# Head outputs brought to feature rows by DMA, and query/key rows laid in quarters, in a fused attention and coupling-net kernel

## The chip, the cores and the metric

One core of one Trainium2 chip runs the whole program. The metric is device time in microseconds (us), as the median of the runs shown. Five engines run their own instruction streams and meet at semaphores: PE (TensorE), ACT (ScalarE), DVE (VectorE), POOL (GpSimd), and SP (SyncE), which here does nothing but issue DMAs and wait.

## What is computed

The input x is 16 batches of 1024 tokens with 256 features. For each batch:

```python
x = x + layernorm(attention(layernorm(x)))      # 16 heads of 8 features, on the first 128 features
x = x + layernorm(coupling(layernorm(x)))

# attention: q, k, v = left @ W.T ; energy = q.k / 4 ; att = softmax over keys ; out = att @ v ; out @ Wo.T + bo
# coupling, 3 cycles, gf from the mean over tokens:
#   tf  = sigmoid(gelu(gelu(gelu(out@w1+b1)@w2+b2)@w3+b3)@w4+b4)
#   out = out + (0.1 + ar * (0.7*gf + 0.3*tf - 0.5) * 2) * twist(out)
```

The weights of the projections are scaled up, so the softmax needs its row maxima, and q and k are split into three bf16 parts each (high, middle, low) to keep fp32 accuracy on the bf16 path of PE.

## The kernel before, in words

The main loop runs b from -2 to 17 over batches, in the same order on each engine. Each turn has two stages, and they are software-pipelined over batches.

**Attention stage of batch b**, 64 steps (`STEPS`), that is 8 groups of 8 steps. A group is one half of the queries (h) and four heads (g). In a step PE computes transposed scores for four heads (L409, bf16, contraction over 48 rows of split parts and 3 rows that carry minus the row maximum), ACT takes the exponential of them (L599, two instructions of 128x1024), and PE weighs the values with them (L424). Column 9 of each head's values is one, so the sum of the exponentials comes out beside the 8 features. At the end of a group ACT copies the 128x512 result to `headsT` (`take_heads`, L608): partition 32*i+d holds feature d of head i of the group, partition 32*i+8 its sum.

**Coupling stage**, 30 beats (`BEATS`). Beat j runs one layer of the coupling net of batch b-1 on PE and its activation on ACT (three cycles of ten layers, `coupling`, `layer_out`). Between them stand, at hand-written beats: for batch b+2 the layernorm (`STATS0`, `NORM0`), projections (`PROJECT_QK`, `PROJECT_V`) and the split into parts; for batch b the way from `headsT` to the projected output (`HEADS`, `TURN_TOK`, `WO`), its layernorm, and the turn into `state`; for batch b-2 the turn back, layernorm and store (`BACK`, `STATS3`, `NORM3`, `ADD_OUT`).

**The way from headsT to the output projection** (batch b, beats 0 to 7): `turn_heads` transposes eight token tiles, four 128x128 fp32 transposes each (L453). For each tile `divide` on DVE takes a reciprocal of the 16 sums (L843) and multiplies the tile with them (L847). `turn_tok` transposes the tiles back (L461, two halves of four), `take_tok` on ACT copies them to `feat_h` (L664), and `project_out` multiplies with `wo` (L468).

**The maxima.** For every query block of every head the row maximum is found ahead of its attention: a *unit* is one matmul 48x128 by 48x512 (L391) and one maximum over 512 columns on DVE (L814). There are 256 units in a batch, 32 in a group. They run as filler: 3 in each attention step (4 in batch 0), and as `BEAT_UNITS` says in the beats, 20, 23 and 21 in the three cycles. They lead the attention by `LEAD` = 112 units, batch 0 by `LEAD0` = 52, which are done before the first attention starts. After a group's 32 units DVE joins and POOL cuts the maxima into three bf16 parts (L963 to L966), and SP transposes them by DMA and writes them into `q_rows` (`lay_max_rows`: one DMA transpose, a wait for its landing, four DMAs), when unit 32(gi+1)+`LAY_AFTER` passes. The scores of a group wait for them (`max_rows_laid`).

**The rows.** `q_rows` and `k_rows` hold the split parts, 8 rows for each of 6 terms, on partitions 0 to 47 (side 0) and 64 to 111 (side 1). They are laid from `parts` by DMA: `lay_row`, L278, one DMA in each of the first 48 steps of the attention before, 64 KB each. The first batch's are laid in `lay_first_rows`: 36 DMAs from SP (L291) and 12 from ACT (L645), in halves of eight heads; the first unit waits for the first half (24 DMAs).

SP's program is one queue in program order: rows, maxima, loads and stores of x. A wait in it holds back everything behind it. The rest of PE's PSUM banks go round as a ring (`ring_bank`): 3 in attention, 5 in the coupling stage, shared by the units and all small results.

## Time and profile before

| | us |
|---|---|
| median of 3 runs | 3556.51 (3555.34 to 3559.84) |
| the profiled execution's own time | 3557.75 |
| its span in the trace | 3555.8 |

```profile
PE   4999999999999999999999999999999999999996
DVE  5998989888898988989888897988989888898821
ACT  2767979798897979889798897979889797896974
PEclk6998999999999999999999999999999999999998
```

The digits are the busy share of 40 equal slices of the span in tenths, and in PEclk the clock granted to TensorE in tenths of full speed. The kernel has a short opening, then a pattern that repeats every 212 us or so (an attention stage of about 130 us, a coupling stage of about 82 us), and an end in which only the coupling net of the last two batches is left.

### The profile page before, as it was taken

To read this page: it belongs to the slowest core of one execution; us is meant where nothing else is said; L and a number is where in the kernel's file an instruction comes from. 1 tells how busy PE (TensorE), PEld (TensorE's weight loads), DVE (VectorE), ACT (ScalarE), POOL (GpSimd) and SP (SyncE) were. 2 spreads that over 40 slices of the span, in tenths; PEclk is the share of its full clock that TensorE was granted. 3 is DMA by queue.
4 is the path that set the end of the run, shared out by engine and by line. 5 is a ranking of instruction groups with operands and counts; after the bars stand their busy time and mean duration, and the time that the engine had idled before them with its cause. 6 is when DMAs were issued, how large, how long until landed. Compare 5 with 4: busy or idle time off the path is not lost.

```text
span 3555.8 us, 56168 instructions
## 1 busy us (share of the span) xinstructions
PE 3379.5 (95%) x19968; PEld 1008.8 (28%) x19968; DVE 2981.2 (84%) x5677; ACT 2931.5 (82%) x3868; POOL 972.2 (27%) x1353
## 2 busy tenths in 40 slices
PE   4999999999999999999999999999999999999996
PEld 1222232323324232232323224232232323223232
DVE  5998989888898988989888897988989888898821
ACT  2767979798897979889798897979889797896974
POOL 3002050421505133060421405033050422404034
PEclk6998999999999999999999999999999999999998
DMA  3101102021211202111020211202111020211001
GB/s 85 27 24 44 33 30 34 26 54 23 51 26 33 54 18 55 30 45 32 26 54 22 51 37 27 49 26 46 30 48 28 26 55 22 44 32 26 3 24 36
DMA packets 71957, 127.89 MB, mean 36 GB/s; under 512 B 37120, under 2 KB 38528, under 8 KB 63616
## 3 DMA queue, kind: packets, MB, share of 16 engines
q1 hardware_dynamic: 68896, 106.75, 12.8%
q0 software_dynamic: 2304, 16.78, 2.6%
q8 instruction: 160, 2.62, 0.3%
q10 hardware_dynamic: 480, 0.79, 0.1%
q14 instruction: 117, 0.96, 0.1%
HBM read 34.61 MB, written 33.55 MB: 19 GB/s over the span
## 4 chain that ended last, share of the span: by engine, by line
PE 72%; DVE 10%; ACT 9%; issue 4%; POOL 2%; DMA 0%; SPq 0%; ACTq 0%; POOLq 0%; DVEq 0%
PE heads_ps L424 24%; PE ring_ps L391 15%; PE scoresT_ps L409 11%; PE scoresT_ps L521 10%; DVE max_parts L814 8%; ACT p_sb L599 4%; PE scoresT_ps L526 3%; DVE stats L825 1%; ACT headsT L608 1%; PE ring_ps L453 1%; PE scoresT_ps L529 1%; PE scoresT_ps L532 1%; POOL y_sb L985 1%; PE scoresT_ps L391 1%; POOL couple L1008 1%
## 5 line engine op out<-in xcount | busy, mean ns | idle before, releaser
L814 DVE TENSOR_REDUCE max_parts<-ring_ps 128x1 f32<-128x512 f32 x3704 | 2343.5, 684 | 269.5 <-PE ring_ps L391 210.5
L599 ACT ACTIVATE p_sb<-scoresT_ps 128x1024 f32<-128x1024 f32 x2048 | 1969.8, 1024 | 103.3 <-PE scoresT_ps L409 79.5
L424 PE MATMUL heads_ps<-p_sb,v_sb 128*9 128x512 f32 x8192 | 1080.4, 599 | 17.9 <-ACT headsT L608 11.9
L391 PE MATMUL ring_ps<-k_rows,q_rows 48*128 48x512 bf16 x3704 | 1074.6, 387 | 17.7 <-DVE max_parts L814 6.3
L409 PE MATMUL scoresT_ps<-q_rows,k_rows 51*128 51x512 bf16 x4096 | 1030.5, 386 | 18.7 <-ACT p_sb L599 9.1
L391 PEld LDWEIGHTS ring_ps<-k_rows,q_rows 48*128 48x128 bf16 x3704 | 263.2, 94 | 1272.6 <-DVE max_parts L814 1177.6
L963 POOL CAST max_wide<-max_all 128x16 bf16<-128x16 f32 x128 | 25.3, 198 | 1709.4 <-DVE max_all L820 1706.7
L521 PE MATMUL scoresT_ps<-state,w 128*128 128x512 f32 x768 | 383.6, 623 | 4.0 <-DVE state L865 2.0
L719 ACT ACTIVATE p_sb<-scoresT_ps,b 128x512 f32<-128x512 f32 x192 | 131.7, 686 | 210.7 <-PE scoresT_ps L521 210.5
L409 PEld LDWEIGHTS scoresT_ps<-q_rows,k_rows 51*128 51x128 bf16 x4096 | 209.4, 94 | 253.4 <-ACT p_sb L599 221.0
L424 PEld LDWEIGHTS heads_ps<-p_sb,v_sb 128*9 128x9 f32 x8192 | 124.5, 88 | 292.1 <-issue 281.6
L526 PE MATMUL scoresT_ps<-p_sb,w 128*128 128x512 f32 x384 | 189.2, 615 | 12.8 <-ACT p_sb L719 11.3
L985 POOL TENSOR_TENSOR y_sb<-y_sb,bo 128x512 f32<-128x512 f32 x64 | 87.5, 1368 | 412.8 <-ACT y_sb L669 412.8
L521 PEld LDWEIGHTS scoresT_ps<-state,w 128*128 128x128 f32 x768 | 132.2, 191 | 170.6 <-issue 162.2
L814 DVE TENSOR_REDUCE max_parts<-scoresT_ps 128x1 f32<-128x512 f32 x187 | 126.7, 678 | 46.3 <-PE scoresT_ps L391 46.3
L721 ACT ACTIVATE p_sb<-scoresT_ps,b 128x512 f32<-128x512 f32 x96 | 66.0, 687 | 98.8 <-PE scoresT_ps L526 98.7
L612 ACT ACTIVATE x_in<-x_in,offset,rstd 128x128 f32<-128x128 f32 (+1 forms) x256 | 123.9, 537 | 22.8 <-POOL offset L973 14.1
L814 DVE TENSOR_REDUCE max_parts<-heads_ps 128x1 f32<-128x512 f32 x205 | 139.1, 678 | 0.4 <-PE heads_ps L391 0.4
L825 DVE BATCH_NORM_STATS2 stats<-x_in 128x6 f32<-128x256 f32 x256 | 94.6, 413 | 37.9 <-ACT x_in L689 29.3
L532 PE MATMUL scoresT_ps<-p_sb,w_all 64*128 64x512 f32 x192 | 102.2, 612 | 13.3 <-ACT p_sb L723 13.3
L1016 POOL TENSOR_TENSOR state<-state,couple 128x512 f32<-128x512 f32 x64 | 98.9, 1546 | 34.7 <-DVE couple L857 34.2
L971 POOL TENSOR_TENSOR rstd<-rstd,minus_half 128x8 f32<-128x8 f32 x64 | 106.9, 1670 | 5.3
(166 smaller groups left out, 2869.5 us busy)
## 6 DMA issues: line engine op xcount, KB each, us to landing
q_rows<-parts SPq DMA_DIRECT2D x378, 64.0 KB
k_rows<-parts SPq DMA_DIRECT2D x378, 64.0 KB
x_sb<-in_x SPq DMA_DIRECT2D x16, 1024.0 KB, 4.8
out<-x_sb SPq DMA_DIRECT2D x16, 1024.0 KB, 3.9
out<-x_in POOLq DMA_DIRECT2D x16, 1024.0 KB, 7.9
x_in<-in_x SPq DMA_DIRECT2D x15, 1024.0 KB, 5.4
q_rows<-max_rows SPq DMA_DIRECT2D x512, 3.0 KB
max_rows<-max_wide SPq DMA_TRANSPOSE x128, 2.3
```

The costliest lines, as they stand in the source:

```text
L391: e.matmul(ring_bank(max_taken, u + 1), q_rows[rows, slot, pair, h * BANK + qb * P:h * BANK + (qb + 1) * P], k_rows[rows, slot, pair, kh * ...
L409: m = e.matmul(scoresT_ps[:, (2 * two + side) * BANK:(2 * two + side + 1) * BANK], k_rows[rows, slot, pair, kb * P:(kb + 1) * P], q_rows[r ...
L424: m = e.matmul(heads_ps[32 * j:32 * j + DH + 1, :], v_sb[:, b % 2, kb, 4 * (group % NG) + j, 0:DH + 1], p_sb[:, n % 2, j, :], start=(kb == ...
L521: o = e.matmul(ps, w1[:, k, m * P:(m + 1) * P], state[:, b % 2, k, c * BANK:(c + 1) * BANK], start=(k == 0), stop=(k == 1))
L526: o = e.matmul(ps, w2[:, k, :], p_sb[:, 0, 2 * c + k, :], start=(k == 0), stop=(k == 1))
L532: o = e.matmul(ps, w4_all[:, :], p_sb[0:D // 2, 1, 2 + c, :], start=True, stop=True)
L599: e.activation(p_sb[:, n % 2, 2 * two:2 * two + 2, :].rearrange("p h n -> p (h n)"), scoresT_ps[:, 2 * two * BANK:(2 * two + 2) * BANK], A ...
L612: m = e.activation(dst(t), src(t), ACT.Identity, bias=offset[i][:, t:t + 1], scale=rstd[i][:, t:t + 1])
L719: e.activation(p_sb[:, 0, 2 * c + m, :], ps, ACT.Gelu, bias=b1[:, m:m + 1]).then_inc(hid_done, 1)
L814: e.tensor_reduce(max_parts[:, gi % 2, kh, col:col + 1], bank_of(max_taken, u + 1), AX.X, ALU.max).then_inc(max_taken, 1)
L825: m = e.bn_stats(stats[i][:, t, :], src(t))
L985: e.tensor_tensor(y_sb[:, rows, :], y_sb[:, rows, :], bo[:, :].unsqueeze(1).to_broadcast([P, 2, E]), ALU.add).then_inc(y_done, 1)
```

## The change

- **Heads.** `turn_heads`, `turn_tok`, `take_tok` and the eight `divide` steps go. SP copies the features from `headsT` straight into `feat_h` by DMA after each group (`lay_heads`, four DMAs of 16 KB, five when the half is complete: the fifth gathers the 32 KB of sums into `sums_in`). At beat `INVERT` = 2 DVE takes one reciprocal of 64x256. SP spreads the result over the partitions (`lay_sums`, four DMAs of 128 KB written). At beats `DIVIDE` = 4, 5 DVE multiplies the two halves of `feat_h`, 128x512 each. The rows of `wo` are permuted on the host to match. `WO` moves from beats 3, 4, 6, 7 to 5, 5, 6, 6.
- **Rows.** They are laid in quarters (four heads) instead of halves: `lay_row` issues 96 DMAs of 32 KB in 64 steps instead of 48 of 64 KB in 48 steps. The units wait for their own quarter.
- **Opening.** `lay_first_rows` goes by quarters: 54 DMAs from SP, 18 from ACT, 24 from POOL. The first unit waits for the first quarter (18 from SP, 6 from ACT). `LEAD0` goes from 52 to 60, and these units stand in beats 5 to 20 instead of 5 to 29.
- **Schedule.** `BEAT_UNITS` gives 18, 24 and 22 units to the cycles; `LAY_AFTER` goes from 3 to 6. `BACK`, `STATS3`, `ROOT3`, `NORM3`, `ADD_OUT`, `ROOT0`, `ROOT1`, `NORM1`, `ADD1` and the second twist (`TWIST1`) stand one or two beats earlier; `STATE` two later, `PROJECT_V` two and three later, `ROOT2` one later.

```diff
-LAY_AFTER = 3
+SUM_PARTS = 2
+SUM_ROWS = H * SUM_PARTS
+LAID = 16 * (2 * H + NH)
+LAY_AFTER = 6
...
-BEAT_UNITS = (3, 2, 2, 1, 3, 2, 2, 2, 2, 1,
-              2, 2, 2, 3, 3, 2, 2, 4, 2, 1,
-              2, 1, 2, 3, 4, 2, 2, 2, 2, 1)
+BEAT_UNITS = (4, 1, 2, 1, 2, 1, 2, 2, 1, 1,
+              2, 3, 2, 3, 3, 2, 2, 4, 2, 1,
+              2, 1, 2, 3, 4, 2, 2, 2, 3, 1)
-LEAD0 = 52
+LEAD0 = 60
+ACT_GROUPS, POOL_GROUPS = (0, 1), (2, 3)
-LAST_BEAT, LAST_STEP = 28, 0
+LAST_BEAT, LAST_STEP = 27, 1
-STATS0, ROOT0, NORM0, TURN_X = (0, 1, 2, 3), 4, (5, 6, 7, 8), (8, 9)
-PROJECT_QK, SPLIT, PROJECT_V = (17, 18, 23, 24), (20, 21, 26, 27), (20, 26)
+STATS0, ROOT0, NORM0, TURN_X = (0, 1, 2, 3), 3, (5, 6, 7, 8), (8, 9)
+PROJECT_QK, SPLIT, PROJECT_V = (17, 18, 23, 24), (20, 21, 26, 27), (22, 29)
-BACK, STATS3, ROOT3, NORM3, ADD_OUT = (10, 11, 12, 13), (11, 12, 13, 14), 15, (17, 18, 19, 25), 27
-HEADS, TURN_TOK, WO, STATS1, ROOT1 = (0, 0, 0, 0, 1, 2, 3, 4), (1, 5), (3, 4, 6, 7), (4, 5, 7, 8), 9
-NORM1, ADD1, STATS2, ROOT2 = (11, 12, 13, 14), (12, 13, 14, 15), (14, 16, 17, 18), 18
-NORM2, STATE = (21, 22, 23, 24), (24, 25, 26, 27)
-GLOBAL = (1, 3, 5)
-TWIST0, UPDATE0, TWIST1, UPDATE1 = 6, 7, 10, 10
+BACK, STATS3, ROOT3, NORM3, ADD_OUT = (8, 9, 10, 11), (10, 11, 12, 13), 14, (16, 17, 20, 24), 26
+INVERT, DIVIDE, WO, STATS1, ROOT1 = 2, (4, 5), (5, 5, 6, 6), (6, 6, 7, 7), 7
+NORM1, ADD1, STATS2, ROOT2 = (10, 11, 12, 13), (11, 12, 13, 15), (14, 16, 17, 18), 19
+NORM2, STATE = (21, 22, 23, 24), (26, 27, 28, 29)
+GLOBAL = (0, 3, 5)
+TWIST0, UPDATE0, TWIST1, UPDATE1 = 6, 7, 9, 10
...
+            def lay_heads(b, group):
+                h, g = divmod(group, NG)
+                e.wait_ge(heads_evac, GROUPS * b + group + 1)
+                if b and group == 0:
+                    e.wait_ge(wo_done, 4 * b)
+                    e.wait_ge(divided, 2 * b)
+                if g == NG - 1:
+                    e.dma_start(sums_in[SUM_ROWS * h:SUM_ROWS * (h + 1), :],
+                                headsT[DH:P:32, h, :, :]).then_inc(heads_laid, 16)
+                for i in range(4):
+                    at = 32 * i + DH * g
+                    e.dma_start(feat_h[at:at + DH, h * BANK:(h + 1) * BANK],
+                                headsT[32 * i:32 * i + DH, h, g, :]).then_inc(heads_laid, 16)
+            def lay_sums(b):
+                e.wait_ge(inverted, b + 1)
+                for h in range(NH):
+                    for k in range(SUM_PARTS):
+                        at = h * BANK + k * BANK // SUM_PARTS
+                        rows = sums_in[SUM_ROWS * h + k:SUM_ROWS * (h + 1):SUM_PARTS, :]
+                        e.dma_start(sums_h[:, at:at + BANK // SUM_PARTS],
+                                    rows.unsqueeze(1).to_broadcast([H, DH, BANK // SUM_PARTS])).then_inc(sums_laid[h], 16)
...
-                    if 0 <= b < N - 1 and n < 48:
-                        lay_row(b + 1, n)
+                    if 0 <= b < N - 1:
+                        for at in range(3 * n // 2, 3 * (n + 1) // 2):
+                            lay_row(b + 1, at)
+                    if valid(b) and n and n % NT == 0:
+                        lay_heads(b, n // NT - 1)
                 for j in range(BEATS):
+                    if valid(b) and j == 0:
+                        lay_heads(b, GROUPS - 1)
+                    if valid(b) and j == INVERT:
+                        lay_sums(b)
...
+            def invert(b):
+                e.wait_ge(heads_laid, LAID * (b + 1))
+                e.reciprocal(sums_in[:, :], sums_in[:, :]).then_inc(inverted, 1)
+            def divide(b, h):
+                half = feat_h[:, h * BANK:(h + 1) * BANK]
+                e.wait_ge(sums_laid[h], 16 * SUM_PARTS * (b + 1))
+                e.tensor_tensor(half, half, sums_h[:, h * BANK:(h + 1) * BANK], ALU.mult).then_inc(divided, 1)
```

## Rows read from the trace of the kernel before

**Rows 1.** The page, part 1: busy time, share of the span, instructions.
```profile
PE 3379.5 (95%) x19968; PEld 1008.8 (28%) x19968; DVE 2981.2 (84%) x5677; ACT 2931.5 (82%) x3868; POOL 972.2 (27%) x1353
```
**Rows 2.** Busy time by stretch: stretch, length, engines, PEclk, DMA share, GB/s.
```profile
1152.00:1283.00 131.00, 129.00 (x956) 27.12 (x956) 121.74 (x199) 126.41 (x138) 16.16 (x34) 0.99 0.24 50
1283.00:1365.00 82.00, 79.28 (x300) 34.91 (x294) 64.94 (x158) 57.29 (x107) 44.49 (x52) 1.00 0.06 18
```
**Rows 3.** The same view: the three cycles of that stage, then two late ones.
```profile
1283.90:1312.90 29.00, 28.81 (x123) 14.57 (x119) 21.41 (x57) 16.15 (x31) 11.05 (x13) 1.00 0.00 1
1312.90:1338.70 25.80, 24.93 (x82) 9.89 (x83) 25.11 (x65) 18.62 (x34) 18.06 (x20) 1.00 0.11 43
1338.70:1364.60 25.90, 24.50 (x92) 10.40 (x90) 17.15 (x34) 22.11 (x45) 15.06 (x19) 1.00 0.06 7
3402.30:3427.40 25.10, 24.23 (x101) 13.44 (x98) 8.23 (x24) 12.86 (x22) 7.98 (x7) 1.00 0.00 1
3470.70:3490.50 19.80, 17.63 (x43) 6.69 (x43) 1.39 (x2) 9.05 (x16) 11.35 (x10) 0.95 0.10 20
```
**Rows 4.** Groups of instructions by line and shape: busy, mean ns, idle before.
```profile
L453 PE MATMUL ring_ps<-ident,headsT 128*128 128x128 f32 x380 | 52.8, 275 | 0.0
L843 DVE RECIPROCAL recip<-ring_ps 128x16 f32<-128x16 f32 x95 | 24.4, 257 | 78.0 <-PE ring_ps L453 74.8
L847 DVE TENSOR_TENSOR tok_h<-ring_ps,recip 128x128 f32<-128x128 f32 x95 | 27.7, 292 | 3.3
L865 DVE TENSOR_TENSOR state<-state,couple 128x512 f32<-128x512 f32 x64 | 44.2, 691 | 15.3 <-POOL couple L1008 12.3
```
**Rows 5.** Timeline at one coupling stage's start: start, us, engine, line, count.
```profile
1284.01 0.60 ACT L608 ACTIVATE headsT<-heads_ps 128x512 f32<-128x512 f32 x1 [1.17 <-PE heads_ps L424]
...
1285.69 1.47 PE L453 MATMUL ring_ps<-ident,headsT 128*128 128x128 f32 x12
...
1287.00 0.60 PE L453 MATMUL scoresT_ps<-ident,headsT 128*128 128x128 f32 x4
...
1287.54 0.39 PE L391 MATMUL heads_ps<-k_rows,q_rows 48*128 48x512 bf16 x1
```
**Rows 6.** Waits of SP's queue: who, for whom, us in total, times, longest.
```profile
SPq L256 <- POOL max_wide L966: 1645.4, 128, 33.6
```
**Rows 7.** Timeline of SP's queue within an attention stage.
```profile
1230.80 1.12 SPq L256 DMA_TRANSPOSE max_rows<-max_wide  x1
1233.12 3.02 SPq L263 DMA_DIRECT2D q_rows<-max_rows  x4
1236.18 7.17 SPq L278 DMA_DIRECT2D q_rows<-parts  x10
```
**Rows 8.** DMA issues: line, engine, count, KB each, median us to landing.
```profile
x_sb<-in_x SPq DMA_DIRECT2D x16, 1024.0 KB, 4.8
max_rows<-max_wide SPq DMA_TRANSPOSE x128, 2.3
```
**Rows 9.** Timeline of the opening, from the first row DMA to the first exponential.
```profile
24.03 2.35 SPq L291 DMA_DIRECT2D q_rows<-parts  x3
...
38.37 0.68 ACTq L645 DMA_DIRECT2D k_rows<-parts  x1
...
51.22 0.67 SPq L291 DMA_DIRECT2D k_rows<-parts  x1
...
52.15 0.60 PE L391 MATMUL scoresT_ps<-k_rows,q_rows 48*128 48x512 bf16 x1 [25.25 <-DMA k_rows<-parts]
...
87.95 1.02 ACT L599 ACTIVATE p_sb<-scoresT_ps 128x1024 f32<-128x1024 f32 x1 [3.09 <-PE scoresT_ps L409]
```
**Rows 10.** Busy time by stretch: the 52 opening units, attention 0, the stage behind.
```profile
52.10:87.90 35.80, 33.36 (x87) 10.31 (x87) 30.15 (x51) 8.80 (x16) 9.94 (x12) 0.50 0.31 62
87.90:250.60 162.70, 152.09 (x1014) 33.80 (x1013) 159.66 (x267) 127.76 (x135) 6.72 (x32) 0.97 0.12 29
250.60:307.20 56.60, 47.12 (x176) 20.10 (x175) 49.90 (x126) 26.18 (x56) 27.87 (x36) 0.73 0.11 39
```
**Rows 11.** Groups by line: a DMA issued from POOL.
```profile
L1088 POOL DMA_DIRECT2D out<-x_in x16 | 15.3, 954 | 29.0 <-ACT x_in L612 29.0
```

More of the change, by code:

```diff
@@ L286, in lay_first_rows @@
                         if i:
[L288 to L292 removed]
+                            e.wait_ge(const_pool, 4)
+                            e.wait_ge(ones_laid, 1)
+                        for side in range(2 if (g, part) == (0, 0) else 1):
+                            for n in (n for n, term in enumerate(TERMS) if term[i] == part):
+                                top, source = 64 * side + DH * n, 64 * side + 16 * g
+                                e.dma_start((q_rows, k_rows)[i][top:top + DH, 0, 2 * g:2 * g + 2, :],
+                                            parts[source:source + 16, i, part, :]).then_inc(rows_laid[0][g], 16)
             for i in range(4):
@@ L340, in sync_program @@
                         load_x(1)
[L341 to L343 removed]
+                        for g in range(NG):
+                            lay_first_rows(g)
                     if valid(b) and j == 0:
@@ L446, in project_v @@
                 m.then_inc(v_done, 1)
-            def turn_heads(b, t):
-                h = t // TPH
-                e.wait_ge(heads_evac, b * GROUPS + (h + 1) * NG)
-                ps = misc_bank(divided, NT * b + t + 1)
-                for g in range(NG):
-                    m = e.transpose(ps[:, g * P:(g + 1) * P], headsT[:, h, g, t % TPH * P:(t % TPH + 1) * P],
-                                    ident[:, :])
-                m.then_inc(headT_done, 1)
-            def turn_tok(b, h):
-                e.wait_ge(divided, NT * b + (h + 1) * TPH)
-                ps = misc_bank(feath_ready, 2 * b + h + 1)
-                for t in range(h * TPH, (h + 1) * TPH):
-                    m = e.transpose(ps[:, t % TPH * P:(t % TPH + 1) * P], tok_h[:, t, :], ident[:, :])
-                m.then_inc(tokT_done, 1)
             def project_out(b, j):
-                e.wait_ge(feath_ready, 2 * b + j // 2 + 1)
+                e.wait_ge(divided, 2 * b + j // 2 + 1)
                 ps = misc_bank(y_taken, 4 * b + j + 1)
@@ L578, in tensor_program @@
                     if valid(b):
-                        if j in TURN_TOK:
-                            turn_tok(b, TURN_TOK.index(j))
-                        for t in range(NT):
-                            if j == HEADS[t]:
-                                turn_heads(b, t)
-                        if j in WO:
-                            project_out(b, WO.index(j))
+                        for i in range(4):
+                            if j == WO[i]:
+                                project_out(b, i)
                         if j in STATE:
@@ L626, in take_qk @@
                     slot = (b - 1) % 2
-                    for half in range(2):
-                        e.wait_ge(rows_laid[slot][half], 24 * 16 * ((b - 1) // 2 + 1))
+                    for g in range(NG):
+                        e.wait_ge(rows_laid[slot][g], laid(b - 1, g))
+                        if g in POOL_GROUPS:
+                            e.wait_ge(pool_laid[g], 12 * 16)
                 if i == 1:
@@ L634, in take_qk, with lay_first_rows @@
                 e.activation(parts[:, i, 0, cols], ps, ACT.Copy).then_inc(qk_evac, 1)
-            def lay_first_rows():
-                for part in range(3):
+            def lay_first_rows(g):
+                for part in range(0 if g else 1, 3):
                     for i in range(2):
@@ L999, in split_low, with lay_first_rows @@
                                 ALU.subtract).then_inc(low_done, 1)
+            def lay_first_rows(g):
+                e.wait_ge(low_done, 4)
+                e.wait_ge(ones_laid, 1)
+                for i in range(2):
+                    for n in range(len(TERMS)):
+                        e.dma_start((q_rows, k_rows)[i][64 + DH * n:64 + DH * n + DH, 0, 2 * g:2 * g + 2, :],
+                                    parts[64 + 16 * g:80 + 16 * g, i, TERMS[n][i], :]).then_inc(pool_laid[g], 16)
             def twist(b, cycle, c):
@@ L1089, in gpsimd_program @@
                     if valid(b):
-                        if j in WO:
-                            add_bias(b, WO.index(j))
+                        for i in range(4):
+                            if j == WO[i]:
+                                add_bias(b, i)
                         if j == ROOT1:
```

97 lines of the change are left out of this document (41 added, 56 removed).

## The prediction

> **What bounds the kernel now.** I read the busy shares first: PE 95%, DVE 84% [rows 1]. An average over unlike stages says little, so the next view is the busy time by stretch. In an attention stage of 131 us PE is busy for 129.0, ACT for 126.4, DVE for 121.7; in the 82 us coupling stage PE for 79.3, DVE for 64.9, ACT for 57.3 [rows 2]. Attention is the longer stage, but the change takes nothing from PE there. The coupling stage is where it works, so I cut that stage into its three cycles [rows 3]. The first third (29.0 us) is PE alone: 28.8 busy against 21.4 on DVE. The second (25.8 us) has DVE busy for 25.1, PE for 24.9: DVE is the bound there, or very near. The third (25.9 us) has PE at 24.5, with gaps in which PE waits for the next activation of the coupling net's own chain. The last two rows of [rows 3] say how far such a cycle can shrink: with the head turns but no units and no projections of a later batch the first cycle takes 25.1 us, and with nothing but the coupling net and the small global net 19.8. Within the first third, twelve and then four transposes of `turn_heads` stand between 1285.69 and 1287.54 [rows 5]. SP is idle for long times: 1645 us of its queue's time is waiting for POOL's cut of the maxima [rows 6]. In the opening the first unit on PE waits for row DMAs until 52.15 [rows 9].
>
> **The heads, PE's side.** Sixteen transposes take 1.85 us (1285.69 to 1287.54), 0.116 each by their spacing, not the 275 ns of a single one, which overlap [rows 4, 5]. A batch has 32 of them and 8 of `turn_tok` of the same shape: 40 x 0.116 = 4.6 us of PE in each first third. WO's matmuls stay. Two `turn_back` (4 transposes each, 0.46 us) move from the second third into the first: +0.9 there. Two units fewer, at 0.2 to 0.39 us each (0.39 is one with its fill, [rows 5]): -0.4 to -0.8. So some 4.2 us less PE work of 28.8. Not all of it becomes time: from the two early-stage rows, 19.8 us with little filler and 29.0 with all of it, PE busy 17.6 and 28.8, so (29.0-19.8)/(28.8-17.6) = 0.82 us of time for 1 us of PE work [rows 3]. That is -3.4 us.
>
> **The heads, the new chain.** In its place stands: copy of the last `headsT` (ends 0.74 us after the stage's first matmul, which was at 1283.87) [rows 5], five DMA issues, landing, reciprocal, four issues, landing, multiply. SP issues ten row DMAs in 7.17 us, 0.72 each [rows 7]. A small DMA lands 2.3 us after its issue starts (the transpose); the 1 MB one 4.8 [rows 8]. Counted from the first matmul of the stage: issues start at 0.9, the last starts at 3.8, has landed by 6.5 (by the two landings, 6.1 and 8.6). DVE is then still at the five units and three statistics of beats 0 to 2, until about 8, so the reciprocal waits for nothing; but if SP is late by over 1.5 us, DVE stands still. The reciprocal's price is not in the trace at this size. Lower bound: 256 elements at the rate of the 128x512 multiply, 691/512 = 1.35 ns each, 0.35 us and a start of 0.1. Upper bound: sixteen times the 257 ns of the one with 16 elements, 4.1 us. The 128-element multiply at 292 ns leaves 0.12 for the start (292 - 128 x 1.35), so the 16-element reciprocal spends 0.137 on 16, 8.6 ns each, and 256 cost 2.2 + 0.1 = 2.3 us; this I take [rows 4]. It ends at 10.4; `lay_sums` issues two DMAs per half: the first half has landed at 11.2 + 2.3 = 13.5 (up to 16 if 128 KB lands like the 1 MB load), the second 1.4 later. Multiplying: 0.7 us per half. PE reaches WO at about 14 by the sum of its work in beats 0 to 5: a wait of 0.3 to 0.8 us is likely. I add 0.6.
> On the Trainium skill's page VectorE: DVE Perf Modes, section on the 8-slice pipeline, reciprocal is an iterative division with a repeat count of 8. At eight times 1.35 ns its 256 elements would cost 2.8 us instead of 2.3, and the sum would be worse by 0.5 us a batch; my two rows point the same way but don't measure it.
>
> **DVE's side.** Out: 8 x (0.257 + 0.292) = 4.4 us a batch [rows 4]. In: 2.3 + 2 x 0.7 = 3.7. Even, in a third where DVE has 7.6 us to spare. ACT loses two copies. Nothing comes of either.
>
> **The units and the moved steps.** The second third gets one unit more, and DVE is its bound. A unit costs DVE 0.636 us (162.7 us for 256 in attention 0, DVE busy 98%) [rows 10]: +0.6. The second twist moved to beats 9 and 19 leaves one in and one out; its wait for the coupling's scaling is now in front of the next beat's unit, cover: five banks of units. `STATE` and `PROJECT_V` move into beats 26 to 29, where PE has its gaps (1.4 us in this third): up to -1.4, less one unit more: -0.2 taken.
> Sum of a full stage: -3.4 + 0.6 + 0.6 - 0.2 = -2.4; with the gaps better filled at either end -3.2. I take -2.7 and keep -5 and +0.5 for the range. Fourteen coupling stages lie between attention 1 and attention 15: -38 us.
>
> **SP's queue.** It gets 48 row DMAs and 38 head and sum DMAs more in each batch. In eight attention steps (16.1 us): 12 rows x 0.72 = 8.6, one `lay_heads` 4 x 0.72 = 2.9, and in six of eight intervals a `lay_max_rows` of 1.12 + 1.2 wait + 3.0 = 5.3 [rows 7]. Together 16.8 where there is one, 11.5 where there is none. So SP is nearly full, and each `lay_heads` ties it to the steps by its wait for `heads_evac`; queued behind that wait are rows and, what counts, the maxima. The tightest is group 7's: it is issued in step 50, behind `lay_heads` of group 5 (free about 1 us into step 48) and three rows: landed at 1 + 2.9 + 2.2 + 5.3 + 2.3 = 13.7 us after step 48 began, and scores need it at 16.1. Margin 2.4 us, cost nothing. At the stage's end SP is 1 to 2 us late at worst, which the 1.5 us of cover for the reciprocal just takes. The load of `x_sb` goes behind `lay_heads` and is needed ten beats later. The earlier `ADD_OUT` frees SP at the stage's start about one beat sooner.
> The Trainium skill's page DMA: Bandwidth & Descriptors (Bandwidth) speaks against this part: transfers under 64 KB are dominated by their descriptors (measured there on loads from HBM, which these are not), and this change cuts 64 KB pieces into 32 and adds ones of 16. By that rule each half-size transfer would cost nearly the same, which is also what I get from the issue time; what it would do here is the first rival below.
>
> **The opening.** 18 SP issues and 6 ACT issues stand before the first unit, instead of the first halves' 24 that were issued by 39.05 and waited for until 52.15 [rows 9]. SP's 18 take 24.0 to about 37 (the wait for the split parts is inside), landing with some of the backlog that made 13 us before: 39 to 44. I take 41: first unit 11 us earlier. 60 units at 0.6 and the projections of batch 1 behind them instead of between them (about 7 us of PE at 1.2 GHz, the granted clock 0.50 of [rows 10], DVE dry for 4 of it): the first exponential at 86.5 instead of 87.95, -1.4, with 8 units more done. Attention 0 is DVE-bound and keeps its 256 units. The stage behind has 52 units instead of 60: 8 x 0.636 = -5.1, but it has no coupling net to fill the time, so the new chain (heads landed at 6.5, sums at 13.5) shows: DVE stands still for 3 to 5 us. -1 taken, -6 and +3 kept. POOL issues 24 DMAs at 0.954 [rows 11], 23 us, after `row_rstd`; the next it has to do is the cut of group 0 at about 60, and it is free by 58. Worth up to 3 us if late.
>
> **The end.** The stage behind attention 15 has beats of 2 us, so the sums come late: of the 4.6 us nearly all is given back to the wait; -1. The rest is unchanged.
>
> **Sum.** -38 - 1.4 - 1 - 1 = -41 from 3557.75 gives 3516.4 for such an execution; the median lies 1.2 below it: **3515**.
>
> **Rivals.** (a) *SP's queue is the new bound*, slower. If a row or head DMA costs not 0.72 but over about 0.85, the intervals with maxima take 19 us of 16.1, and the last `lay_heads` starts 3 us late. DVE then waits at the reciprocal, PE at its ring banks; each us late is a us per stage, 15 times. At 0.95 (POOL's price) 4 more us late, minus the 2.7 gained: about +1.5 x 15, 3578. For: SP is full by count. Against: the four small ones of 3 KB cost 0.72 too, so the price hardly depends on the size, and a smaller one should not cost more. 12%. (b) *The sums are late everywhere*: landing of 128 KB spread costs 4.8 and the reciprocal 4.1; PE waits 3 us more at WO, and of 2.7 nothing to 1 is left: 3545 to 3555. 15%. (c) *The first quarter isn't early*: the transfers are bound by the data path, not by the issue; the opening gives nothing or loses 4: 3521. 10%, within the forecast's range. (d) *More of the saved PE time counts*, -4.2 a stage, and the third cycle's gaps close: 3490. 15%. (e) The forecast itself, 3503 to 3530: 48%.
>
> A measurement here can tell about 0.2% (7 us) from no change. Faster by over that: (c), (d), (e) and most of (b): 0.82. Within: 0.05. Slower: 0.13. The range: from 3486 (d) to 3549 (b).
>
> **What would show it.** Right: no L453 and L461 rows; the first cycle at 25.5 to 26.5 us instead of 29.0, the second at 26 to 26.5, the third at 25 to 26; attention stages unchanged at 129 to 131.5; the reciprocal at 2.3 us; the first unit at 41. Wrong: a wait of L409 for a DMA at step 56 or attention stages over 132 us (a), DVE idle before the reciprocal or before the multiply by more than 1 us, PE idle before L468 (b), or more half-clock stretches at attention starts, since PE has less to do in the first third.

## The result and the profile after

The changed kernel takes 3465.98 us (median of 4 runs, 3463.11 to 3468.58) against 3555.93 us of the kernel before (median of 4): ratio 0.9745, 95% interval 0.9728 to 0.9762. It is 90 us faster. The forecast was 41 us, and its range ended at 3486: right in its sign, and less than half of what came.

The page of the profiled execution (busy time, clock by slices):

```profile
span 3462.1 us, 55776 instructions
PE 3286.2 (95%) x19328; PEld 932.0 (27%) x19328; DVE 2938.1 (85%) x5469; ACT 2911.6 (84%) x3836; POOL 986.1 (28%) x1377
...
PEclk7998999999999999999999999999999999999998
```

PE has 93.3 us less to do (3379.5 in [rows 1]) and the span is 93.7 us shorter: PE's share stays at 95%. The same views by stretch as [rows 2] and [rows 3]: an attention stage, the coupling stage behind it, its three cycles, and the first cycle of the last two nets. A cycle ends here, as in [rows 3], where ACT starts the activation of the cycle's last layer (stretch, length, PE, PEld, DVE, ACT, POOL busy, PEclk, DMA share, GB/s):

```profile
1123.00:1254.40 131.40, 129.54 (x966) 28.61 (x965) 122.40 (x201) 128.01 (x143) 14.46 (x33) 1.00 0.17 42
1254.40:1331.30 76.90, 74.06 (x260) 30.14 (x260) 61.96 (x144) 56.08 (x106) 47.99 (x54) 1.00 0.20 53
1255.40:1281.60 26.20, 24.63 (x87) 10.92 (x84) 20.28 (x52) 15.24 (x29) 11.98 (x13) 1.00 0.25 71
1281.60:1304.90 23.30, 22.88 (x77) 8.50 (x76) 22.65 (x53) 18.04 (x33) 16.59 (x20) 1.00 0.12 47
1304.90:1329.60 24.70, 23.93 (x84) 9.71 (x84) 17.39 (x38) 21.09 (x39) 17.72 (x21) 1.00 0.17 29
3312.70:3335.30 22.60, 20.62 (x65) 9.53 (x62) 8.45 (x21) 12.00 (x21) 8.78 (x8) 1.00 0.27 75
3374.70:3395.40 20.70, 18.00 (x51) 6.90 (x50) 1.81 (x4) 9.20 (x17) 10.85 (x10) 1.00 0.03 5
```

The first cycle went from 29.0 to 26.2, the second from 25.8 to 23.3, the third from 25.9 to 24.7. Unrounded the three shrink by 6.3 us together, but the stage from 82.2 to 76.95, by 5.3 only: between the last activation and the first exponential of the attention 0.57 us became 1.62. ACT there, before:

```profile
1364.50 0.67 ACT L733 ACTIVATE couple<-scoresT_ps,b_half 128x512 f32<-128x512 f32 x1
1365.07 1.93 ACT L599 ACTIVATE p_sb<-scoresT_ps 128x1024 f32<-128x1024 f32 x2
```

and after, with the copies of the values and of the last state now in between:

```profile
1329.73 0.68 ACT L756 ACTIVATE couple<-scoresT_ps,b_half 128x512 f32<-128x512 f32 x1
1330.30 0.60 ACT L686 ACTIVATE v_sb<-heads_ps 128x512 f32<-128x512 f32 x1
1330.78 0.60 ACT L705 ACTIVATE state<-scoresT_ps 128x512 f32<-128x512 f32 x1
...
1331.34 1.95 ACT L627 ACTIVATE p_sb<-scoresT_ps 128x1024 f32<-128x1024 f32 x2
```

The mean of the fourteen full coupling stages, part by part:

| part of a full stage | before | after | difference | forecast |
|---|---|---|---|---|
| last exponential to first matmul | 1.03 | 1.03 | 0 | 0 |
| first cycle | 28.96 | 26.15 | -2.8 | -3.4 + 0.6 |
| second cycle | 25.54 | 23.30 | -2.2 | +0.6 |
| third cycle | 25.79 | 24.64 | -1.15 | -0.2 |
| last activation to next exponential | 0.57 | 1.58 | +1.0 | 0 |
| better filled gaps at either end | | | | -0.3 |
| stage | 81.89 | 76.70 | -5.2 | -2.7 |

Laid end to end by the first and last exponential of each batch, the two spans differ so:

| stretch | before | after | difference | forecast |
|---|---|---|---|---|
| start to first exponential | 87.9 | 86.3 | -1.6 | -1.4 |
| attention 0 | 162.7 | 158.6 | -4.1 | 0 |
| stage behind attention 0 | 56.6 | 53.4 | -3.2 | -1 |
| attention 1 to 15 together | 1947.6 | 1939.5 | -8.1 | 0 |
| the 14 full coupling stages | 1146.4 | 1073.8 | -72.6 | -38 |
| behind attention 15 | 154.5 | 150.4 | -4.1 | -1 |
| span | 3555.8 | 3462.1 | -93.7 | -41 |

The full coupling stages hold 35 of the 53 us that were missed, attention 0 to 15 another 12. DVE's timeline around the edge between the first and second cycle of a stage, before:

```profile
1309.83 0.75 DVE L825 BATCH_NORM_STATS2 stats<-y_sb 128x6 f32<-128x256 f32 x2 [1.16 <-POOL y_sb L985]
...
1313.41 0.74 DVE L825 BATCH_NORM_STATS2 stats<-y_sb 128x6 f32<-128x256 f32 x2
1314.18 0.64 DVE L835 BATCH_NORM_AGGREGATE moments<-stats 128x2 f32<-128x6 f32 x8
...
1317.89 1.43 DVE L857 TENSOR_TENSOR couple<-couple,state 128x512 f32<-128x512 f32 x1
```

and after, where the second cycle begins at 1281.6:

```profile
1263.02 1.73 DVE L862 RECIPROCAL sums_in<-sums_in 64x256 f32<-64x256 f32 x1
...
1267.84 0.69 DVE L867 TENSOR_TENSOR feat_h<-feat_h,sums_h 128x512 f32<-128x512 f32 x1
...
1269.65 0.68 DVE L867 TENSOR_TENSOR feat_h<-feat_h,sums_h 128x512 f32<-128x512 f32 x1
...
1279.09 0.75 DVE L847 BATCH_NORM_STATS2 stats<-y_sb 128x6 f32<-128x256 f32 x2 [0.50 <-POOL y_sb L1007]
1279.87 0.64 DVE L857 BATCH_NORM_AGGREGATE moments<-stats 128x2 f32<-128x6 f32 x8
```

Before, the statistics of the attention output ended inside the second cycle (which began at 1312.9), in front of its units. After, they end before it. The reciprocal waits for nothing here (no bracket behind it), and PE's first two WO products at 1270.16 stand right behind the small global net (`hg`, 1269.86): the new chain costs PE no wait in this stage. SP's queue in the same stage:

```profile
1222.17 0.67 SPq L317 DMA_DIRECT2D k_rows<-parts  x1
1224.56 2.67 SPq L292 DMA_DIRECT2D feat_h<-headsT  x4
...
1253.52 4.30 SPq L317 DMA_DIRECT2D q_rows<-parts  x6
1257.87 0.58 SPq L288 DMA_DIRECT2D sums_in<-headsT  x1
1258.49 2.69 SPq L292 DMA_DIRECT2D feat_h<-headsT  x4
1261.29 0.38 SPq L396 DMA_DIRECT2D x_sb<-in_x  x1
```

From 1224.56 to 1261.67 it has no gap over 0.15 us except the landing of the maxima. The last heads' DMAs start at 1257.87, 2.4 us after the stage's first matmul (1255.43), because row DMAs stand in front of them. The heads were ready 0.7 us after that matmul.

### The profile page after: what moved, and what is told of

Same layout as the page of the kernel before. It is cut to its first block, busy times and chain, and to the rows that moved or that the text cites. A ratio compares the mean times of both kernels' runs of the same rounds, so it can differ in the third digit from the quotient of the medians.

```text
span 3462.1 us, 55776 instructions
## 1 busy us (share of the span) xinstructions
PE 3286.2 (95%) x19328; PEld 932.0 (27%) x19328; DVE 2938.1 (85%) x5469; ACT 2911.6 (84%) x3836; POOL 986.1 (28%) x1377
## 3 DMA queue, kind: packets, MB, share of 16 engines
q1 hardware_dynamic: 93072, 124.03, 13.6%
## 4 chain that ended last, share of the span: by engine, by line
PE 71%; DVE 13%; ACT 9%; issue 4%; SPq 2%; POOL 1%; DMA 1%; POOLq 0%; DVEq 0%
PE heads_ps L472 24%; PE ring_ps L439 15%; PE scoresT_ps L457 11%; DVE max_parts L836 10%; PE scoresT_ps L553 8%; ACT p_sb L627 4%; PE scoresT_ps L558 3%; PE scoresT_ps L561 2%; DVE stats L847 2%; PE scoresT_ps L564 1%; ACT headsT L636 1%; PE ring_ps L500 1%; PE scoresT_ps L486 1%; PE heads_ps L439 1%; ACT p_sb L742 1%
## 5 line engine op out<-in xcount | busy, mean ns | idle before, releaser
L439 PE MATMUL ring_ps<-k_rows,q_rows 48*128 48x512 bf16 x3741 | 1078.1, 385 | 24.1 <-DVE max_parts L836 14.2
L472 PE MATMUL heads_ps<-p_sb,v_sb 128*9 128x512 f32 x8192 | 1073.9, 596 | 17.9 <-ACT headsT L636 11.9
L985 POOL CAST max_wide<-max_all 128x16 bf16<-128x16 f32 x128 | 25.1, 196 | 1769.1 <-DVE max_all L842 1769.1
L836 DVE TENSOR_REDUCE max_parts<-scoresT_ps 128x1 f32<-128x512 f32 x144 | 97.9, 680 | 36.0 <-PE scoresT_ps L439 35.9
L561 PE MATMUL scoresT_ps<-p_sb,w 128*64 128x512 f32 x192 | 101.9, 612 | 15.3 <-ACT p_sb L744 13.7
L992 POOL TENSOR_SCALAR rstd<-moments 128x8 f32<-128x8 f32 x64 | 23.5, 367 | 303.2 <-DVE moments L857 300.0
```

The lines of the kernel that those rows point to most:

```text
L439: e.matmul(ring_bank(max_taken, u + 1), q_rows[rows, slot, pair, h * BANK + qb * P:h * BANK + (qb + 1) * P], k_rows[rows, slot, pair, kh * ...
L472: m = e.matmul(heads_ps[32 * j:32 * j + DH + 1, :], v_sb[:, b % 2, kb, 4 * (group % NG) + j, 0:DH + 1], p_sb[:, n % 2, j, :], start=(kb == ...
L561: o = e.matmul(ps[0:D // 2, :], w3[:, :], p_sb[:, 1, c, :], start=True, stop=True)
L836: e.tensor_reduce(max_parts[:, gi % 2, kh, col:col + 1], bank_of(max_taken, u + 1), AX.X, ALU.max).then_inc(max_taken, 1)
```

## The experiments

Below, "stage" is a full coupling stage, from the last exponential of one batch to the first of the next, and "attention" an attention stage. Both are the median over the batches, 76.9 and 129.0 us in the changed kernel. Cycles are read as above; one turn is one batch. A time of a single run is called so.

**The old beats in the changed kernel.**

```diff
-BEAT_UNITS = (4, 1, 2, 1, 2, 1, 2, 2, 1, 1,
-              2, 3, 2, 3, 3, 2, 2, 4, 2, 1,
-              2, 1, 2, 3, 4, 2, 2, 2, 3, 1)
+BEAT_UNITS = (3, 2, 2, 1, 3, 2, 2, 2, 2, 1,
+              2, 2, 2, 3, 3, 2, 2, 4, 2, 1,
+              2, 1, 2, 3, 4, 2, 2, 2, 2, 1)
-BACK, STATS3, ROOT3, NORM3, ADD_OUT = (8, 9, 10, 11), (10, 11, 12, 13), 14, (16, 17, 20, 24), 26
+BACK, STATS3, ROOT3, NORM3, ADD_OUT = (10, 11, 12, 13), (11, 12, 13, 14), 15, (17, 18, 19, 25), 27
-NORM2, STATE = (21, 22, 23, 24), (26, 27, 28, 29)
+NORM2, STATE = (21, 22, 23, 24), (24, 25, 26, 27)
...
```

> The changed kernel with the beats of the kernel before put back (BEAT_UNITS, GLOBAL, BACK, STATS3, NORM3, ROOT0, NORM1, ADD1, STATE, PROJECT_V, TWIST1, LAST_BEAT); head outputs still go by DMA, rows still in quarters, and DIVIDE, WO, STATS1, ROOT1 stay at their new beats since they hang on the new chain. Theory T (the saving of 5.3 us a coupling stage has several sources: PE's 40 transposes, about 2.8 us in the first cycle; DVE's statistics of the attention output taken before the second cycle instead of within it, about 1.5 us there; the new beats of the turn back, twist, state and values, about 1.5 us in all): stage of 78 to 79 us instead of 76.9, total 3485 to 3500. Rival R (removing the head turns alone carries it, the new beats are only tidying): stage 76.9 to 77.3, total within 7 us of 3466. Rival S (the new beats carry most of it): stage 80 or more, total 3510 or more.

3493.89 us, ratio 0.9827 (0.9812 to 0.9842). Stage 78.4: theory T's place. But the parts were not as T had them: the first cycle fell to 24.9, by 4.1 us, and the second stayed at 26.05 although the statistics stood early. Its three cycles:

```profile
1885.71:1910.60 24.89, 24.22 (x84) 10.38 (x81) 20.50 (x54) 14.91 (x29) 11.61 (x13) 1.00 0.26 73
1910.60:1936.65 26.05, 24.92 (x82) 9.75 (x83) 23.75 (x56) 18.62 (x33) 17.39 (x21) 1.00 0.11 43
1936.65:1962.50 25.85, 24.44 (x93) 10.46 (x91) 17.11 (x35) 22.06 (x44) 15.00 (x19) 1.00 0.06 7
```

In the second cycle DVE's work fell from 25.1 [rows 3] to 23.75 and the time did not follow: PE has 24.9 there. So in the kernel before DVE was not the only bound of that cycle.

**The new beats in the kernel before.**

```diff
-BACK, STATS3, ROOT3, NORM3, ADD_OUT = (10, 11, 12, 13), (11, 12, 13, 14), 15, (17, 18, 19, 25), 27
+BACK, STATS3, ROOT3, NORM3, ADD_OUT = (8, 9, 10, 11), (10, 11, 12, 13), 14, (16, 17, 20, 24), 26
...
```

> The kernel before (head turns on PE, rows in halves, old opening) with the new beats alone: BEAT_UNITS, GLOBAL, BACK, STATS3, NORM3, ADD_OUT, ROOT0, NORM1, ADD1, ROOT2, STATE, PROJECT_V, TWIST1, LAST_BEAT; WO and STATS1 stay at their old beats. Theory T: first cycle 29.5 (two turns back move in), second 25 to 25.8 (its DVE still begins with the last statistics of the attention output), third 24.7: stage of 80.5 to 81.5, total 3530 to 3548. Rival R: no gain, total 3550 to 3560. Rival S: stage of 79 or less, total 3515 or less.

3571.74 us, ratio 1.0047 (1.0030 to 1.0064): slower by 16 us, outside all three expectations. The second and third cycle shrink about as T said (24.9 and 24.75), but the first grows to 31.0:

```profile
1925.84:1956.80 30.96, 29.25 (x127) 15.21 (x124) 21.23 (x59) 16.23 (x31) 11.45 (x13) 1.00 0.00 1
```

With the head turns still in it, that cycle doesn't take the two turns back without loss. The fourteen stages get 24.5 us longer in all, while attention 1 to 15 gets 11.6 us shorter (1936.0 against 1947.6); in six of these stages the granted clock also fell to 1.2 GHz for 3.4 us some 8 us in, which it did in none before. Set side by side, the heads (and rows) alone give -62 us, the beats alone +16, both together -90. The beats are worth -28 where PE has been emptied first. One difference goes with the heads in this account: `WO` and the statistics behind it are early in the first of these two runs and late in the second, since they hang on the new chain.

**The same, with the global net at its old beats.** I took the crowded beat 0 (6.45 us instead of 4.17) for the cause.

```diff
-GLOBAL = (0, 3, 5)
+GLOBAL = (1, 3, 5)
```

> The kernel before with the new beats alone, as in the run that was 16 us slower, but with the global net at its old beats 1, 3, 5. Theory G (the new beat 0 is too full beside four head turns: global net and five units ask for ring banks that DVE frees one by one, PE idle 1.5 us at 4.7 us): beat 0 at 4.2 to 5.3 us instead of 6.45, first cycle 29 to 30 instead of 31.0, total 3540 to 3560. Rival: it is the two turns back moved into a cycle where PE is full anyway: first cycle 30.5 or more, total above 3563.

3573.35 us in one run, first cycle 30.98 again, beat 0 at 6.05. My theory G fell; the rival's numbers came. What remains different in that cycle are above all the turns back and the order of the units, and no run separates these two.

**The statistics late.**

```diff
-INVERT, DIVIDE, WO, STATS1, ROOT1 = 2, (4, 5), (5, 5, 6, 6), (6, 6, 7, 7), 7
+INVERT, DIVIDE, WO, STATS1, ROOT1 = 2, (4, 5), (5, 5, 6, 6), (7, 8, 9, 9), 9
```

> The changed kernel with the statistics of the attention output on DVE moved from beats 6, 6, 7, 7 to 7, 8, 9, 9 and ROOT1 from 7 to 9, nothing else. Theory T (the second cycle is bound by DVE, and it got shorter because these statistics no longer run over into it): second cycle 24.5 to 25.3 us instead of 23.3, stage 78 to 79. Rival R: DVE is not what counts there, cycles change by under 0.4 us.

3485.02 us (one run, 19 above). First and third cycle unchanged (26.2, 24.75), second 24.6 instead of 23.35, stage 78.2. The second cycle:

```profile
1284.03:1308.63 24.60, 22.97 (x77) 8.41 (x76) 23.42 (x62) 18.07 (x33) 16.73 (x18) 1.00 0.11 45
```

PE has as little to do as in the changed kernel (22.9), DVE 0.8 us more: DVE's side does count in the second cycle once PE is out of the way, as theory T said.

**The turns back late.**

```diff
-BACK, STATS3, ROOT3, NORM3, ADD_OUT = (8, 9, 10, 11), (10, 11, 12, 13), 14, (16, 17, 20, 24), 26
+BACK, STATS3, ROOT3, NORM3, ADD_OUT = (10, 11, 12, 13), (11, 12, 13, 14), 15, (17, 18, 19, 25), 27
```

> The changed kernel with BACK, STATS3, ROOT3, NORM3, ADD_OUT at the old beats only. Theory T (the second cycle has PE and DVE both full, and moving two turns back out of it took 0.9 us of PE from it, put into the first where PE has idle places): first cycle 25.2 to 25.6 instead of 26.2, second 24.8 to 26 instead of 23.3, stage 77.5 to 78.3. Rival U (the second cycle is shorter for the earlier twist or the statistics alone): second cycle within 0.4 us of 23.3 and the stage shorter than 76.9.

3489.15 us (one run, 23 above). Second cycle 26.1, first 25.85, third 24.0, stage 78.6: rival U falls, and the effect is a little larger than theory T's ranges. The second cycle:

```profile
1906.86:1932.97 26.11, 24.74 (x83) 9.71 (x84) 24.12 (x56) 18.62 (x34) 17.69 (x21) 1.00 0.11 43
```

PE 24.7 instead of 22.9 us, but DVE too has 24.1 instead of 22.65. Put together, the runs give the second cycle in all four cases:

| second cycle, us | turns back late | turns back early |
|---|---|---|
| statistics late | 25.8 (before) | 24.6, and 24.9 with the head turns on PE |
| statistics early | 26.1, with all old beats 26.05 | 23.35 (changed kernel) |

The early statistics alone give nothing, the early turns back alone about 1 us, both together 2.45. That both groups of steps were needed is shown. That the turns back work through PE is argued from PE's busy time alone: their own statistics and norms moved with them, and no run moved the four transposes by themselves. The size depends a little on the marks. Counted from a cycle's first matmul to the next cycle's, the second cycle goes from 24.05 to 22.3, with 24.03 and 24.06 for the early statistics alone; of PE's 2.0 us less, some 0.9 are two matmuls of the next cycle's first layer, which stood in front of the mark on ACT before and stand behind it now.

**State and values at the old beats.**

```diff
-PROJECT_QK, SPLIT, PROJECT_V = (17, 18, 23, 24), (20, 21, 26, 27), (22, 29)
+PROJECT_QK, SPLIT, PROJECT_V = (17, 18, 23, 24), (20, 21, 26, 27), (20, 26)
-NORM2, STATE = (21, 22, 23, 24), (26, 27, 28, 29)
+NORM2, STATE = (21, 22, 23, 24), (24, 25, 26, 27)
```

> The changed kernel with STATE at 24 to 27 and PROJECT_V at 20, 26 as before, nothing else. Theory T (these two, moved to the last beats, fill the places where PE waited for activations; the third cycle is shorter by that, and PE's busy last beats keep its granted clock up at the attention's start): third cycle 25.7 to 26 instead of 24.7; half-clock stretches at attention starts come back, 8 to 11 instead of 3 after the first 300 us, attention stages 1 to 15 together 1946 to 1951 instead of 1939. Rival V (the clock's stretches have another cause, and come and go by chance): attention sum within 3 us of 1939.

3478.66 us (one run, 13 above). Third cycle 26.6, above theory T's range, but the stage only 77.7, since the way from the last activation to the next exponential is 0.57 us again instead of 1.62. So these two steps are worth 0.8 us of a stage, not the 1.8 of the third cycle. The attention stages 1 to 15 take 1947.1 together instead of 1939.5, as before. The 3 us ahead of an attention stage and its first 8 us, in this kernel:

```profile
1330.20:1333.20 3.00, 2.40 (x11) 0.69 (x10) 2.81 (x5) 2.84 (x6) 2.92 (x4) 1.00 1.02 213
...
1333.00:1341.00 8.00, 7.28 (x43) 1.44 (x47) 6.27 (x11) 6.62 (x8) 7.84 (x7) 0.79 0.60 183
```

and in the changed kernel:

```profile
1328.30:1331.30 3.00, 2.98 (x19) 1.57 (x17) 1.97 (x4) 2.99 (x8) 2.92 (x3) 1.00 1.05 218
...
1331.30:1339.30 8.00, 7.31 (x54) 1.69 (x54) 7.33 (x13) 7.78 (x11) 7.19 (x7) 1.00 0.52 162
```

With PE busy for 2.40 of the last 3 us, the granted clock falls to 1.2 GHz for 3.4 us at this attention's start (43 PE instructions in 8 us instead of 54); with 2.98 it stays at 2.4. Of the starts of attention 1 to 15, 9 have such a stretch in this kernel, 8 in the kernel before and 10 with all the old beats. In the changed kernel it is 3, and in every other run here that has the two steps at their new places 0 to 4, also where the rest is the kernel before. An attention stage without a stretch takes 129.0 us as a rule, one with it mostly 130 to 132. Each count is from one profile, but all three kernels with the old places sum to 1947.1 to 1950.2 us over attention 1 to 15, and all with the new ones to 1936.0 to 1941.2, leaving out the two in which the scores wait for their maxima (below). So rival V falls: it is these two steps. Not each gap brings a stretch. In the kernel before, PE is busy for 2.1 to 2.2 of the last 3 us ahead of each attention, and the clock falls at 8 of the 15; what decides that isn't shown.

**The rows in halves, the opening as before.**

```diff
-LEAD0 = 60
+LEAD0 = 52
...
-                        for at in range(3 * n // 2, 3 * (n + 1) // 2):
-                            lay_row(b + 1, at)
+                    if 0 <= b < N - 1 and n < 48:
+                        lay_row(b + 1, n)
```

> The changed kernel with the rows laid as before: 48 DMAs of 64 KB a batch, the opening's 48 from two queues in halves, 52 units ahead in beats 5 to 29; head outputs by DMA and all new beats stay. Theory T: the quarters are worth only the opening; coupling stages stay at 76.9, attention at 129.0; first unit at 52, first exponential at 88, 8 units more in the stage behind attention 0: total 6 to 9 us above 3466. Rival Q (the smaller row transfers also matter in the steady state, through shorter transfers in front of the maxima or head transfers): stages change by over 0.5 us. Rival C (the earlier rows are what lets the clock rise early and so shortens attention 0 from 162.7 to 158.6): attention 0 back at 162 or more, total 12 us above.

3468.57 us (3467.80 to 3470.41), ratio 0.9756 (0.9741 to 0.9770). Stage 76.9, attention 129.0: the quarters are worth nothing in the steady state, so rival Q falls. Attention 1 starts at 304.9 instead of 298.3 us, the 6.6 us of theory T; 3.2 of them come back in the attention stages, where this profile has one half-clock stretch instead of three. Attention 0 took 161.2 us, between the two that were expected; the clock rises for good at 95.6 us here, at 92.8 in the changed kernel, at 98.9 before, so rival C holds in part. The total, 2.6 us above 3466, stays under theory T's 6 to 9 by what came back.

**More issues on SP's queue.** Head DMAs cut into two halves of their columns, all four of a group, then one, then two:

```diff
-                    e.dma_start(feat_h[at:at + DH, h * BANK:(h + 1) * BANK],
-                                headsT[32 * i:32 * i + DH, h, g, :]).then_inc(heads_laid, 16)
+                    for c in (0, BANK // 2):
+                        e.dma_start(feat_h[at:at + DH, h * BANK + c:h * BANK + c + BANK // 2],
+                                    headsT[32 * i:32 * i + DH, h, g, c:c + BANK // 2]).then_inc(heads_laid, 16)
```

> The changed kernel with each head DMA cut into two halves of its columns: 32 more DMA issues a batch on SP's queue, about 21 us of issuing, same bytes. It tells how near SP's queue is to being the bound (the first rival of the prediction). Theory T (each eight-step interval of attention has 16.1 us, with maxima 16.2 us of SP's work at 0.64 to 0.71 us an issue; 2.6 more don't fit in the intervals with maxima): the last head DMAs start 3 to 5 us late, DVE waits for them before the reciprocal, stage of 78 to 81 us instead of 76.9; attention stages stay at 129 to 130. If SP had room: stage within 0.4 us of 76.9. If it is far over: attention stages over 131 us, scores waiting for maxima.

> The changed kernel with one of the four head DMAs of each group cut into two: 8 more issues a batch, 5 us on SP's queue (32 more, 21 us, cost 17 us a turn and made the scores wait for the maxima). Theory T (SP's queue is at its edge but not over: in the changed kernel it still waits 1.7 us for the heads of group 5 ahead of the last maxima): 8 more still fit, stage 76.9 to 77.5, attention stages 129 to 130, total up to 3475. Rival: the changed kernel is already over the edge and every issue costs, 0.5 us for each of 8 a turn: total 3510 or more.

> The same with two of the four cut: 16 more issues a batch, 10.5 us of SP's queue. Theory T (a queue that is full costs what it is over): between the two, stage 77 to 79, attention 129 to 133, total 3480 to 3540. If the cliff lies later than 16: within 10 us of 3466.

| issues more a batch | us (one run each but the first) | stage | attention |
|---|---|---|---|
| 0 | 3465.98 | 76.9 | 129.0 |
| 8 | 3506.78 | 79.2 | 129.0 |
| 16 | 3567.52 | 79.7 | 133.6 |
| 32 | 3700.84 | 82.0 | 140.5 |

All three went worse than theory T. With 8 more the total lies just under the rival's 3510, by which every issue costs. With 8 more, DVE waits for the heads in front of the reciprocal:

```profile
1906.73 1.74 DVE L864 RECIPROCAL sums_in<-sums_in 64x256 f32<-64x256 f32 x1 [2.12 <-DMA feat_h<-headsT]
```

SP starts that stage's last head DMAs at 1901.39 (its stage begins at 1896.94), 4.45 us in, against 2.44 in the changed kernel. Two us later in the queue are 2.12 us of waiting here, and 1.6 to 4.0 in the fourteen full stages. The changed kernel has no cover left, and in three of these fourteen it already waits there, for 0.35 to 0.95 us. With 16 and 32 more, the scores of group 7 wait for their maxima too, in fourteen of the attention stages; with 32 (who, for whom, us in total, times, longest):

```profile
PE scoresT_ps L458 <- DMA q_rows<-max_rows: 131.7, 14, 10.7
```

**Units and global net moved.** First three units alone, into PE's idle places:

```diff
-BEAT_UNITS = (4, 1, 2, 1, 2, 1, 2, 2, 1, 1,
+BEAT_UNITS = (3, 2, 2, 1, 2, 1, 2, 3, 1, 0,
               2, 3, 2, 3, 3, 2, 2, 4, 2, 1,
-              2, 1, 2, 3, 4, 2, 2, 2, 3, 1)
+              2, 2, 2, 2, 4, 2, 2, 2, 3, 1)
```

> The changed kernel with three units moved by one or two beats: BEAT_UNITS 3, 2 instead of 4, 1 in beats 0 and 1; 3, 1, 0 instead of 2, 1, 1 in beats 7 to 9; 2, 2 instead of 1 and 3 in beats 21 and 23. PE's idle places in the changed kernel (0.57 us at 2.9 us for a ring bank, 0.46 at 6.0, 0.55 at 22.3 and 0.55 at 54 us, all but the first for an activation) would each be filled by a unit. Theory T (PE's idle places are what is left to gain): stage 75.3 to 76.3 instead of 76.9, total 3445 to 3458. If the chain of activations is the bound there: stage unchanged within 0.3.

3463.64 us, ratio 0.9725 (0.9709 to 0.9741): not to be told from the changed kernel. Stage 76.6: theory T fell, and the stage stayed within the 0.3 us of its rival. An idle place of 1.24 us appeared at the first cycle's end, where PE now waits for DVE to free a ring bank for a unit. Then the global net as well, with the units of beats 7 to 9 left alone:

```diff
-BEAT_UNITS = (4, 1, 2, 1, 2, 1, 2, 2, 1, 1,
+BEAT_UNITS = (3, 2, 2, 1, 2, 1, 2, 2, 1, 1,
               2, 3, 2, 3, 3, 2, 2, 4, 2, 1,
-              2, 1, 2, 3, 4, 2, 2, 2, 3, 1)
+              2, 2, 2, 2, 4, 2, 2, 2, 3, 1)
-GLOBAL = (0, 3, 5)
+GLOBAL = (1, 3, 5)
```

> The changed kernel with the global net back at beats 1, 3, 5 (it is in beat 0 in the changed kernel) and the units 3, 2, 2, 1 instead of 4, 1, 2, 1 at the start of the first cycle, 2, 2 instead of 1 and 3 in beats 21 and 23. Theory T (beat 0 has six users of five ring banks, so PE waits 0.57 us for one, and the next activation comes late): first cycle 25.3 to 25.9 instead of 26.2, stage 75.8 to 76.4, total 3450 to 3460. Rival: the chain of activations sets the pace, and the time is within 4 us of 3466.

3445.73 us (3443.26 to 3449.61), ratio 0.9684 (0.9666 to 0.9702): 20 us faster than the changed kernel, the fastest of all, and a little better than theory T. Its cycles:

```profile
1865.30:1890.20 24.90, 24.10 (x85) 10.64 (x82) 19.65 (x52) 15.26 (x29) 11.54 (x13) 1.00 0.26 73
1890.20:1914.00 23.80, 23.16 (x77) 8.76 (x77) 23.27 (x53) 18.04 (x34) 17.04 (x21) 1.00 0.12 47
1914.00:1938.50 24.50, 23.80 (x84) 9.80 (x85) 17.40 (x37) 21.00 (x40) 17.83 (x21) 1.00 0.17 29
```

PE's idle time in the first cycle falls from 1.57 to 0.80 us, stage 75.9. Against the run just above two things differ, the global net and the units of beats 7 and 9; which of them gives the 18 us between the two is not shown. Here DVE waits for the heads before the reciprocal in five of the fourteen full stages, for 0.5 to 1.5 us: the shorter stage comes nearer to SP's limit.

## Why the prediction was too small

**The transposes.** The 4.6 us of PE a stage held: with the old beats PE's work in the first cycle falls from 28.8 to 24.2, and the time by 4.1, which is 0.89 us for each us of work where I had 0.82. With the new beats, which load the cycle with two turns back, PE's work falls by the 4.2 of the forecast, and the time by 2.8. That is the -3.4 + 0.6 of the sum, but by luck: it is 0.67 for each us of work, and the 0.6 us of wait that I had added was not there.

**The new chain.** Reciprocal 1.73 us instead of 2.3, `sums_h` landed 2.4 us after issue instead of 2.3, WO reached without a wait in the stage shown.

**The second cycle: the step that failed.** The sum had +0.6, since DVE was its bound and one unit came in; measured -2.2 in the mean of fourteen stages, 2.8 us a stage off, 40 us in all. That is more than the 35 us by which these stages were missed; 4 of the difference are the 0.3 a stage that I had granted for filled gaps. The forecast gave the second cycle no relief at all, and it was wrong in two ways. On DVE's side ("Nothing comes of either") I balanced the work by cycle of the code, but in the trace of before DVE ran behind and carried 1.4 us of the attention output's statistics (0.74 and 0.64 for their aggregates) from the first cycle over into the second; the earlier WO and statistics took them out. On PE's side I counted the turns back's 0.9 us only where they arrived, in the first cycle, not where they left, though PE stood at 24.9 of 25.8 us in [rows 3]. The late-statistics and the late-turns runs show that both groups of steps were needed. A smaller term, seen in one place: the twist of 1.43 us at 1317.89 beside the same step on POOL takes 0.68 in the changed kernel at 1283.61, where POOL's comes a us later.

**The third cycle and the clock.** -0.2 was taken of a possible -1.4. The third cycle gave -1.15, but 1.0 of it came back as the longer way to the next exponential, so the stage got -0.15: the term held, for a reason that it did not name. That the same two steps keep PE busy up to the attention's first matmul and so save half-clock stretches, 8 us over attention 1 to 15, I had not seen: I named half-clock stretches at attention starts only as something that could get worse.

**The opening.** First unit at 41.48 us (41 forecast), first exponential at 86.3 (86.5). POOL's 24 issues took 13.6 us, not 23: 0.56 each. Attention 0 got 4.1 us shorter, where nothing was expected; with the rows in halves it is 161.2 us, so the earlier rows hold 2.6 of them. Where the other 1.5 come from, and the 2.2 by which the stage behind it beat its forecast, stays open.

**The end.** The chain behind attention 15 was to give back nearly all, and 4.1 us came instead of 1, since PE's wait was short. DVE in that stage (start, us, idle before and releaser):

```profile
3318.07 1.74 DVE L862 RECIPROCAL sums_in<-sums_in 64x256 f32<-64x256 f32 x1 [36.37 <-DMA feat_h<-headsT]
3323.95 0.69 DVE L867 TENSOR_TENSOR feat_h<-feat_h,sums_h 128x512 f32<-128x512 f32 x1 [4.14 <-DMA sums_h<-sums_in]
```

The first half's product was ready at 3324.6, 11.9 us into the stage, and PE took it at 3324.70, right behind beat 5. Its first cycle fell from 25.1 [rows 3] to 22.6.

**SP's queue.** The rival (a) did not come, but the forecast's calm was luck: the count of 16.8 us in 16.1 was about right, the 1.5 us of cover at the reciprocal was not there. The issue price is by the piece: 0.67 us for a head DMA of 16 KB with the pause behind it (four in 2.69), 0.71 for 32 KB (six in 4.30), 0.72 for 64 KB [rows 7]. What bounds is the queue that issues, not the transfers, whose share of the 16 engines is 13.6%. The Trainium skill's rule on transfers under 64 KB (DMA: Bandwidth & Descriptors, Bandwidth), measured there on loads from HBM and taken over to these, would have made the halved pieces cost the DMA engines nearly as much each as the whole ones. The runs don't bear that out: all transfers of this hardware queue, 124 MB, take 14.4% of the 16 engines' time with the rows in halves and 13.6% with the rows in quarters.

**The range.** Its far end, rival (d) at 3490, had more of PE's saved time count in the first cycle and the third cycle's gaps close. That isn't what carried the time beyond it: the first cycle gave 2.8 us, not 4.2.

## What to carry to other kernels

Where two engines are nearly equally busy in a stretch (24.9 and 25.1 of 25.8 us here), ask of every moved step on both engines where it leaves as well as where it arrives, and read from the timeline, not from the source, in which stretch an engine really does its work. Moves of work and removals don't add: nearly the same schedule cost 16 us on the full cycle and gave 28 on the emptied one. Follow a gain to the stage's end before you book it: the third cycle's 1.15 us was almost all back before the next exponential. A queue that only issues DMAs has a budget of its own, in pieces: count it per interval between its waits, and test how far the cliff is by adding issues.
